# Coupling network on one core: one gelu per slot in layer 2, a slot's eight transposes in a row, and batch 6 attended before the last kv is copied

## What is computed

```
xn  = layernorm(x)                                  x: 8 batches x 512 tokens x 128, fp32
# linear attention and a gated feed-forward network
q, k, v = xn @ Wqkv + bqkv;  qp, kp = elu(q)+1, elu(k)+1
attn = (qp @ (kp^T v)) / (qp . sum(kp) + eps)
x1  = layernorm(xn + attn);  s = layernorm(x1 + (silu(x1 Wg) * (x1 Wu)) Wd)
# coupling network, three cycles
gf  = global_net(mean(xn))
o = xn
for cycle in range(3):
    tf = sigmoid(w4(gelu(w3(gelu(w2(gelu(w1(o))))))))        # 128 -> 128 -> 64 -> 32 -> 1 per token
    o  = o + (0.1 + range * 2 * (0.7 gf + 0.3 tf - 0.5)) * twist(o)
out = x + s * silu(o)
```

## Time and profile before

| | before |
|---|---|
| median of three runs | 164.96 us |
| the profiled execution's own time | 165.76 us |
| its span | 163.2 us |
| mean granted TensorE clock | 0.991 |
| PE busy | 153.9 us (94%) |
| DVE busy | 137.5 us (84%) |
| ACT busy | 132.1 us (81%) |
| POOL busy | 113.0 us (69%) |

### The profile page before, as it was taken

The page is one execution under the profiler, slowest core; times in us unless marked ns, Lnnn a source line. Parts: engine busy times, 40 slices in busy tenths (PEclk is TensorE's granted clock), DMA queues, the critical chain, the costliest instruction groups (busy, mean ns, idle before and its releaser), DMA issues.

```text
span 163.2 us, 3407 instructions
## 1 busy us (share of the span) xinstructions
PE 153.9 (94%) x934; PEld 118.2 (72%) x934; DVE 137.5 (84%) x549; ACT 132.1 (81%) x345; POOL 113.0 (69%) x202
## 2 busy tenths in 40 slices
PE   7979999999999999999999999999999999999930
PEld 7757988888888687454554565788888888888830
DVE  2988699899988989299999968978767999969893
ACT  3889886999999988999999986995648986854950
POOL 0077766789991859993074297379999998896572
PEclk9999999999999999999999999999999999999996
DMA  5997332030330000000000000000000110110113
GB/s 175 256 388 151 64 66 53 16 66 5 61 68 0 2 6 0 0 0 0 4 0 0 8 0 0 0 0 4 0 0 9 58 64 6 64 66 0 64 64 129
DMA packets 11922, 7.83 MB, mean 48 GB/s; under 512 B 8960, under 2 KB 9728, under 8 KB 11904
## 3 DMA queue, kind: packets, MB, share of 16 engines
q1 hardware_dynamic: 11472, 7.28, 15.9%
q10 hardware_dynamic: 432, 0.34, 0.7%
HBM read 3.43 MB, written 2.10 MB: 34 GB/s over the span
## 4 chain that ended last, share of the span: by engine, by line
PE 80%; DVE 7%; ACT 7%; issue 3%; POOL 1%; DVEq 0%; ACTq 0%
PE bank L1068 11%; PE bank L1260 10%; PE bank L1185 7%; PE bank L1249 7%; PE bank L1251 7%; PE bank L1250 7%; PE bank L1197 4%; PE bank L1210 4%; PE bank L1139 3%; PE bank L1150 2%; PE bank L1085 2%; PE bank L1126 2%; PE bank L1130 2%; PE bank L1127 2%; DVE u L724 2%
## 5 line engine op out<-in xcount | busy, mean ns | idle before, releaser
L514 ACT ACTIVATE pq<-bank,bffn 128x512 f32<-128x512 f32 (+1 forms) x24 | 16.1, 682 | 9.3 <-PE bank L1251 9.3
L270 POOL TENSOR_TENSOR rstd<-ve,minus_half 128x4 f32<-128x4 f32 x21 | 21.3, 1013 | 1.8
L814 DVE SCALAR_TENSOR_TENSOR pq<-bank,bffn,pq 128x512 f32<-128x512 f32 (+1 forms) x24 | 17.6, 739 | 5.2 <-issue 2.4
L1249 PE MATMUL bank<-x_hi,ffn_hi 128*128 128x512 f32 (+1 forms) x48 | 20.5, 427 | 0.0
L1250 PE MATMUL bank<-x_lo,ffn_hi 128*128 128x512 f32 (+1 forms) x48 | 18.9, 394 | 0.0
L1251 PE MATMUL bank<-x_hi,ffn_lo 128*128 128x512 f32 (+1 forms) x48 | 18.9, 394 | 0.0
L1260 PEld LDWEIGHTS bank<-wd,pq 128*128 128x128 f32 x144 | 17.9, 191 | 1.2
L1260 PE MATMUL bank<-wd,pq 128*128 128x128 f32 x144 | 18.0, 274 | 0.0
L454 ACT ACTIVATE q_stage<-bank,col 128x512 f32<-128x512 f32 x24 | 16.1, 677 | 0.4 <-PE bank L1068 0.3
L268 POOL TENSOR_SCALAR nm<-mv 128x4 f32<-128x4 f32 x21 | 4.7, 223 | 15.8 <-DVE mv L651 15.6
L322 POOL TENSOR_TENSOR ab<-cpl 128x8 f32<-128x8 f32 x4 | 6.5, 1628 | 12.4 <-ACT cpl L486 12.3
(11 more groups left out here) (174 smaller groups left out, 458.9 us busy)
## 6 DMA issues: line engine op xcount, KB each, us to landing
x_tok<-in_x SPq DMA_DIRECT2D x8, 256.0 KB, 6.8
tx_tok<-xn_tok SPq DMA_DIRECT2D x16, 128.0 KB, 2.4
out<-pq SPq DMA_DIRECT2D x6, 256.0 KB, 2.0
r_tok<-in_w_ffn SPq DMA_DIRECT2D x1, 341.0 KB, 6.7
r_tok<-in_w_first SPq DMA_DIRECT2D x1, 320.0 KB, 3.6
out<-pq SPq DMA_DIRECT2D x2, 128.0 KB, 1.9
out<-pq ACTq DMA_DIRECT2D x1, 256.0 KB, 2.0
row<-in_rows SPq DMA_DIRECT2D x1, 192.0 KB, 6.3
```

Of the source, the lines that this page charges most:

```text
L270: return pool.tensor_tensor(rstd[i][:, b], ve[i][:, b], minus_half[:], ALU.pow)
L514: act.activation(sg[n % 2][0:m], gate_of(n)[0:m], ACT.Silu, bias=bffn[0:m, c:c + 1]).then_inc(sg_ready, 1)
L814: dve.scalar_tensor_tensor(out=hid[b % 2][0:m, c], in0=up_of(n)[0:m], scalar=bffn[0:m, CHUNKS + c:CHUNKS + c + 1], in1=sg[n % 2][0:m], op0 ...
L1249: pe.matmul(dst[0:m], ffn_hi[:, w], x1_hi[:, b], start=True, stop=False)
```

## The change

Three edits, and the semaphore counts that go with them: `gelu_2` is one operation over 512 columns; `layer_1(s + 2)` issues both batches' transposes ahead of `layer_3(s)`; `attend(6)` stands ahead of `copy_kv(7)` on VectorE.

```diff
                 act.wait_ge(h2_ps, s + 1)
                 if s >= 2:
                     act.wait_ge(h3_ps, s - 1)
-                for ch in range(2):
-                    cs = slice(ch * 256, (ch + 1) * 256)
-                    act.activation(h2[:, s % 2, cs], ps_h2[s % 2][:, cs], ACT.Gelu,
-                                   bias=col[:, COL["cn_b2"]:COL["cn_b2"] + 1]).then_inc(h2_ready, 1)
+                act.activation(h2[:, s % 2], ps_h2[s % 2][:], ACT.Gelu,
+                               bias=col[:, COL["cn_b2"]:COL["cn_b2"] + 1]).then_inc(h2_ready, 1)
...
             add_eps(BATCHES - 2)
             invert_den(BATCHES - 2)
+            attend(BATCHES - 2)
             copy_kv(BATCHES - 1)
-            attend(BATCHES - 2)
...
+                pe.wait_ge(h2_ready, s + 1)
                 for ch in range(2):
-                    pe.wait_ge(h2_ready, 2 * s + ch + 1)
                     last = pe.matmul(ps_h3[64 * ch:64 * ch + 64, :], sm("cn_w3"),
...
                 if s >= 1:
                     layer_4(s - 1)
-                layer_1(s + 2, (0,))
+                layer_1(s + 2)
                 layer_3(s)
-                layer_1(s + 2, (1,))
```

More of the change, by code:

```diff
@@ L1182, in layer_2 @@
                 if s >= 2:
-                    pe.wait_ge(h2_ready, 2 * (s - 1))
+                    pe.wait_ge(h2_ready, s - 1)
                 for par in range(2):
@@ L1359, in _ @@
             gate_up(1)
-            pe.wait_ge(h2_ready, 2 * SLOTS)
+            pe.wait_ge(h2_ready, SLOTS)
             gate_up(2)
```

## The result

The change made the kernel slower: 170.08 us median of four runs (168.82 to 170.30) against 165.04 (164.93 to 165.64) for the kernel before, timed beside it. The ratio is 1.0287 (95% interval 1.0255 to 1.0318), 5.0 us. The profiled execution took 170.30 us with a span of 168.4.

A forecast was written before the change was run, and what follows sets the result against it. VectorE, 3.15 us per slot, was taken as the bound, so only filling and drain could gain. 0.43 (layer 2 of slot 11) + 0.15 (gelu) - 0.03 (rounding) = 0.55; 164.96 - 0.55 = 164.4 us, range 163.8 to 165.0.

The forecast's parts named there:

- the 0.24 of the forecast: Mid-loop, TensorE waits ahead of its transposes for next_r, about 0.24 us per slot.
- when coupling(0) is ready: Filling of the loop: ScalarE's coupling(0) was to be ready at 69.0 to 69.25 instead of 69.57.
- I take 0.34: First next_r on VectorE: gain of 0.34 us, its first operation waiting until 69.47 for GpSimd's scale_x1.
- the bound of 0: First next_r: no gain if GpSimd's next operation, 0.41 us at 69.45, also goes first.
- rival 2: Start of the first next_r gains nothing; the drain's 0.09 + 0.15 are left: 164.7 us, within the noise; chance 0.18.
- 0.43: Drain: TensorE's layer 2 of slot 11 starts at 97.52 against 97.95, 0.43 us gained.
- what stands in the way is GpSimd: At the first next_r, GpSimd's scale_x1 (68.20 to 69.47) delays VectorE's first operation; 0.34 us gained, bounds 0 and 0.6.
- VectorE, dense from there: From the first next_r VectorE runs without a hole and ends the last next_r at 94.91 instead of 95.25.
- the four rivals: No GpSimd hindrance 164.1 (0.22); start gains nothing 164.7 (0.18); TensorE bound 162.0 (0.02); slower 165.8 (0.09).
- the slower one: Layer 3 queued behind transposes waiting for VectorE closes a loop; 1.4 us lost against 0.55 gained: 165.8; chance 0.09.

The follow-up runs named there:

- after_breath: Changed kernel plus one VectorE memset of one column per slot, behind minus_s, read by nobody: 164.38 us, 0.9985 of the kernel before.
- the lower level: Changed kernel, unaltered, timed again on chip 3, with L322 held instead of nmr of batch 7: 165.92 us, 1.0070 of the kernel before.
- after_twin: Changed kernel plus one VectorE tensor_tensor of one column per slot, with two SBUF inputs, behind minus_s: 164.65 us, 0.9982 of the kernel before.

## Why the prediction was wrong

**Right: the bound and the sizes of the saved work.** Layer 2 of slots 2 and 3 starts at 73.00 and 76.15, so the slot is VectorE's 3.15 us as said, and TensorE has a wait at its transposes, once per slot, between the two batches. It is 0.39 at 71.93; from the next slot on the eight transposes take 1.31 us with `next_r` in the way and 1.07 in slot 1 without, which is the 0.24 of the forecast. From layer 3 to layer 2 behind it are 0.48 us. On ScalarE the single gelu occupies 67.57 to 68.14, 0.57 against 0.58. TensorE's and ScalarE's timelines after:

```profile
60.58 1.11 PE L1148 MATMUL bank<-kv_sb,q_stage 128*128 128x129 f32 x8
...
71.93 0.66 PE L1066 MATMUL bank<-small,r_tok 128*128 128x128 f32 x4 [0.39 <-DVE r_tok L757]
72.52 0.65 PE L1195 MATMUL bank<-h,small 128*64 128x256 f32 x4
73.00 0.59 PE L1183 MATMUL bank<-q_stage,small 128*64 128x512 f32 x1
...
74.42 1.31 PE L1066 MATMUL bank<-small,r_tok 128*128 128x128 f32 x8
```
```profile
67.57 0.69 ACT L461 ACTIVATE h<-bank,col 128x512 f32<-128x512 f32 x1
68.14 0.28 ACT L473 ACTIVATE tt<-bank,half_b 128x8 f32<-128x8 f32 x1
68.45 0.67 ACT L484 ACTIVATE cpl<-tt,base,gain 128x4 f32<-128x4 f32 x2
```

**Right: when coupling(0) is ready.** It ends at 68.45 + 0.67 = 69.12, within the 69.0 to 69.25 of the forecast. The wait of `numerator(7)` is gone (60.58 instead of 60.99).

**Off in size: the start.** "I take 0.34" for the first `next_r`. VectorE's timeline, its first operation alone:

```profile
69.16 0.88 DVE L757 SCALAR_TENSOR_TENSOR r_tok<-pq,cpl 128x128 f32<-128x128 f32 x1 [2.55 <-ACT cpl L484]
```

It was hindered where I said, but not by `scale_x1` alone: the second operation starts at 69.96, not 69.54. That is 0.08 behind the end of GpSimd's next one (L315, 69.47 + 0.41 = 69.88), which went first as well. I had named this as the bound of 0 and set it aside, because the old `next_r` lost only 0.05 beside L315. That row was misread: the old `next_r` began at 69.61 and its second operation was due 0.26 later, at 69.87, when L315 was over in any case (69.45 + 0.41 = 69.86). The second `next_r` starts at 72.85 against 72.84, so up to here rival 2 came true. `after_breath` shows what it gives where no hold follows: layer 2 of slot 11 starts at 97.89 in it, 0.06 before its old place, not 0.43, and the median is 0.33 us below before, which is not clear of the noise. Without the hold rival 2's 164.7 would have been the right forecast.

The Trainium skill ("SBUF — State Buffer", SBUF: two separate sides) states that of a VectorE operation with two SBUF inputs and a GpSimd operation that reads SBUF the one that starts first keeps the shared pair of ports for its whole length, and the other waits. The 0.88 us agree with it as far as `scale_x1` goes. They don't for L315, which by its record started at 69.47, after the `next_r` operation at 69.16, and went first all the same. What the page says of one pair of operations gives no hint of what a row of ninety does.

**Wrong: the step "what stands in the way is GpSimd".** It weighed what GpSimd's operations do to VectorE, and put what VectorE does to GpSimd at nothing, without a reason. It says "VectorE, dense from there" and draws from it only VectorE's own end. But beside a VectorE without a hole a small GpSimd operation can be shut out until the row ends, for 23.52 us in the profile after; behind it in GpSimd's queue stood `norm_x1(7)`, for which TensorE waits in slot 9, and the scalars for `o3_early`. I had read GpSimd's queue only to 75 us. The rows of 3.36 and 2.64 us at L322, at 82 and 92 us of the trace of before, were the warning: seventeen and thirteen times the 0.20 of their like. None of the four rivals had this mechanism; the slower one had the wrong engine and a price of 1.4 us in place of 5. At the lower level the forecast fails by the same step: 165.92 is over its range of 163.8 to 165.0, and the held operation is L322.

What the edits do to make a hold longer or likelier isn't settled; no run tried it. The kernel before has the same row of operations and shows at most 3.36 us; with each edit alone the one profile has a longer hold (12.96, 6.43, 12.97), and the memset shortened them in both kernels. That the changed kernel is exposed is shown, by a long hold in each of its three profiles; why it fell on `nmr` in two of them and on L322 in one, by chance or by the chip, is not.

## What to carry to other kernels

When an edit fills VectorE with an unbroken row of operations that read two tensors from SBUF, look at every GpSimd operation beside that row, and at who is queued behind it: an instruction of one shape with lengths of 0.2 and 3.4 us in one trace is a warning, even where nobody waits for it yet. Ask for each engine that becomes dense what it does to its neighbours, not only when it ends itself. One memset per slot was a cheap test and a cheap cure, and a wait made on purpose prices a suspected delay in a run of its own. If a kernel's trace holds an operation with such a spread, time it again unaltered, at another time and on another chip, before settling on a size.

## What was new about the hardware

- A GpSimd product of 128x4 or 128x8 numbers, 0.20 us by itself, lasted 12.95 to 12.97 us in six kernels and 23.52 in two profiles of the changed one, each time to the end of VectorE's row. The larger GpSimd operations with one tensor input (L301, 128x128) mostly went on beside the same row at 0.6 us each (2.47 for four), but one of them was held for 3.66 in `after_twin`.
- The long holds of products end at seams of VectorE's row, 0.14 to 0.15 us behind the start of a new group of operations, so their lengths recur (3.4 to 3.5, 4.61, 12.96, 23.52); starts that agree to a few ns led to different ones.
- With a memset of 0.06 us per slot of twelve operations no hold of over 2 us was seen in five profiles, and the memset didn't lengthen the slot. With an operation of 0.15 us and two SBUF inputs in its place one hold was left, 3.66 us, to just behind the next of them.
- After a stop of 3.9 us TensorE was granted 0.71 to 0.78 of its clock over the ten us around it and 0.88 to 0.95 in the next ten; keeping it at work through the stop saved 1.8 us.
